# Copying x to the output as two DMAs of alternate 2 KB rows instead of one DMA of long runs

## The reference, cut to what matters

```python
q, k, v = (silu(causal_conv4(n @ W)) for W in (Wq, Wk, Wv))       # n: x, layer-normed
delta   = delta_rule_chunkwise(q, k, v, beta)                      # recurrent state S over the sequence
ms      = multiscale_conv(v, ms_w3, ms_w15, ms_w31, kernel_mix_w, channel_mixer_w)
wts     = softmax(gelu(features @ fusion_w1) @ fusion_w2)
o       = rmsnorm(wts0 * ms + wts1 * delta + wts2 * v)
att     = o @ Wo
ffn     = sigmoid(mix(n) @ W_r) * (square(relu(mix(n) @ W_k)) @ W_v)
out     = x + att + ffn
```

## Time and profile before

| | |
|---|---|
| median of 3 runs | 3813.25 us (3811.24 to 3821.89) |
| the profiled execution, its own time | 3814.92 us |
| its span, first to last instruction | 3813.1 us |
| PE busy | 3381.8 us, 89% |
| DVE busy | 3159.1 us, 83% |
| ACT busy | 2760.3 us, 72% |
| POOL busy | 760.7 us, 20% |
| granted TensorE clock, mean | 0.936 of full speed |
| one step, from one copy of x to the next | 116.86 us in the step read below |

### The profile page before, as it was taken

The page is one execution under the profiler, slowest core; times in us unless marked ns, Lnnn a source line. Parts: engine busy times, 40 slices in busy tenths (PEclk is TensorE's granted clock), DMA queues, the critical chain, the costliest instruction groups (busy, mean ns, idle before and its releaser), DMA issues.

```text
span 3813.1 us, 69963 instructions
## 1 busy us (share of the span) xinstructions
PE 3381.8 (89%) x22848; PEld 2513.9 (66%) x22848; DVE 3159.1 (83%) x7856; ACT 2760.3 (72%) x9144; POOL 760.7 (20%) x1489
## 2 busy tenths in 40 slices
PE   6898889988889888889888898888898888988877
PEld 5666667666667666667666676666666666766654
DVE  5988889888789888798888898888988888888884
ACT  5676778766777667777767776677776777766774
POOL 2012221112221122211122211222112221112220
PEclk8999999999999999999999999999999999999988
DMA  6012211112211122211222111222112221112220
GB/s 176 13 37 47 47 41 36 27 37 47 47 35 35 24 47 47 42 31 25 42 47 47 35 35 24 47 47 42 32 21 46 47 47 32 34 28 47 41 40 7
DMA packets 188307, 154.92 MB, mean 41 GB/s; under 512 B 111804, under 2 KB 146108, under 8 KB 187688
## 3 DMA queue, kind: packets, MB, share of 16 engines
q0 software_dynamic: 31744, 79.70, 12.2%
q1 hardware_dynamic: 156200, 70.76, 7.1%
HBM read 51.34 MB, written 52.95 MB: 27 GB/s over the span
## 4 chain that ended last, share of the span: by engine, by line
PE 48%; ACT 23%; DMA 15%; issue 8%; DVE 4%; POOL 1%; ACTq 0%; POOLq 0%; DVEq 0%; SPq 0%
DMA my<-prod 14%; PE front L516 6%; PE dense L721 6%; PE dense L674 5%; PE dense L678 5%; PE dense L754 5%; PE dense L662 5%; ACT my L1106 3%; DVE my L1531 2%; PE cell L637 2%; PE small L690 2%; ACT dense L1136 2%; ACT prod L1117 2%; PE cell L644 2%; PE cell L645 1%
## 5 line engine op out<-in xcount | busy, mean ns | idle before, releaser
L1531 DVE SCALAR_TENSOR_TENSOR my<-vT,mw,my 128x256 f32<-128x256 f32 x5408 | 2233.9, 481 | 34.8 <-DMA my<-prod 20.2
L516 PE MATMUL front<-xsh,wk 128*128 128x256 f32 x1024 | 291.0, 448 | 252.7 <-ACT raw L894 252.7
L721 PE MATMUL dense<-xsh,w 128*128 128x256 f32 x2048 | 481.9, 381 | 4.0
L516 PEld LDWEIGHTS front<-xsh,wk 128*128 128x128 f32 x1024 | 232.4, 230 | 306.1 <-ACT raw L894 264.1
L1117 ACT ACTIVATE prod<-vT,mw 128x256 f32<-128x256 f32 x480 | 210.6, 509 | 295.5 <-DMA my<-prod 295.4
L397 POOL TENSOR_SCALAR vare<-xsq 128x2 f32<-128x2 f32 x32 | 6.2, 193 | 2096.8 <-ACT xsh L856 2096.8
L721 PEld LDWEIGHTS dense<-xsh,w 128*128 128x128 f32 x2048 | 368.4, 190 | 72.1 <-ACT xr L1168 11.1
L1507 DVE SCALAR_TENSOR_TENSOR xr<-xsh,rest,xr 128x256 f32<-128x256 f32 x128 | 53.7, 482 | 277.4 <-ACT xk L1072 277.4
L1079 ACT ACTIVATE ka<-dense 128x512 f32<-128x512 f32 x64 | 38.2, 597 | 314.7 <-PE dense L662 314.7
L457 POOL DMA_DIRECT2D my<-prod x160 | 146.4, 915 | 540.0 <-ACT prod L1117 341.0
L662 PE MATMUL dense<-xk,wfk 128*128 128x256 f32 x1024 | 236.8, 385 | 12.0 <-DVE xk L1507 10.1
(11 more groups left out here) (182 smaller groups left out, 7021.9 us busy)
## 6 DMA issues: line engine op xcount, KB each, us to landing
my<-prod POOLq DMA_DIRECT2D x160, 384.0 KB, 4.2
xa<-in_x SPq DMA_DIRECT2D x32, 512.0 KB, 4.5
rows_out<-Bm SPq DMA_DIRECT2D x64, 256.0 KB, 4.2
out<-xb POOLq DMA_DIRECT2D x32, 512.0 KB, 6.1
Yq<-units_out SPq DMA_DIRECT2D x128, 32.0 KB, 3.1
w<-in_w SPq DMA_DIRECT2D x1, 2048.0 KB, 16.5
Bu<-rows_out SPq DMA_DIRECT2D x32, 64.0 KB, 3.1
units_out<-Xu SPq DMA_DIRECT2D x32, 64.0 KB, 2.5
```

What stands on the lines that cost most here:

```text
L516: i = e.matmul(by_batch(front[pair % 2][:, c * W:(c + 1) * W]), wt[:, k, hs(c0 + c)], xsh[s % 2][:, k, :, 1:1 + P], start=(k == 0), stop=( ...
L721: e.matmul(by_batch(o), w1[:, k, hs(2 * pair + c)], xsh[s % 2][:, k, :, 1:1 + P], start=(k == 0), stop=False)
L1531: i = e.scalar_tensor_tensor(o, vT[s % 2][:, c, :, off:off + P], mw[:, col:col + 1], o, ALU.mult, ALU.add)
```

## The change

The copy of one step's rows of x is issued as two DMAs instead of one. Each takes both batches, and of the 128 rows of a batch every second one: the first DMA the even rows, the second the odd rows. A row is 512 floats, 2 KB. The place in SP's program is the same. Both DMAs count up the same semaphore by 16, so `add_out` waits for 32 a step instead of 16.

```diff
@@ copy_x
                 if s >= 2:
                     e.wait_ge(stored[s % 2], s // 2 * 16)
-                e.dma_start(out[:, s * P:(s + 1) * P, :], x[:, s * P:(s + 1) * P, :]).then_inc(x_copied[s % 2], 16)
+                def every_second(t):
+                    return t[:, s * P:(s + 1) * P, :].rearrange("b (p t) d -> t b p d", t=2)
+
+                for t in range(2):
+                    e.dma_start(every_second(out)[t], every_second(x)[t]).then_inc(x_copied[s % 2], 16)
@@ add_out
-                e.wait_ge(x_copied[s % 2], s // 2 * 16 + 16)
+                e.wait_ge(x_copied[s % 2], s // 2 * 32 + 32)
```

## The result

The changed kernel takes 3644.93 us (median of 4 runs, 3640.35 to 3666.02), beside 3814.49 for the kernel before; the ratio is 0.9564, 95% interval 0.9524 to 0.9604. That is 170 us less, where 276 were forecast. The profiled execution took 3647.26, 167.7 less than that of before.

What follows compares the result with a forecast made beforehand. The bound was PE's pause while addition r0 took turns with the copy's 64 KB packets on two engines. 28 steps x 9.4 = 263 plus about 13 for the other four, off 3814.9, gave 3539 (3537 against the median); range 3475 to 3650.

Steps and rivals of the forecast that it cites:

- the forecast's own 3488 to 3606: Whole kernel: bounds around the forecast time, from gains of 11.2 and 7.0 us a step; the forecast had chance 0.66.
- rival 1: Copy's queue: short packets stretch the copy, so `Yq` is late or additions r1 and r2 pay more; 3610 to 3790, chance 0.18.
- the longest landing: Sign at the additions of `prod` onto `my`: longest time from issue to landing falls from 15.9 to some 6 us.
- the clock: Sign at PE: without the long pause the granted clock is near 1.00, against 0.94 in the step with it.
- The turn is one packet for one: Copy's two engines: copy's and additions' queues alternate one packet each, even with many small packets waiting.
- r0 ... pays 8 x 0.088 = 0.7 us: First addition onto `my`: 8 rows an engine each wait one 2 KB packet of 0.088 us, on top of 4.2 us.
- its four turns: Addition r0 before the change: 4 copy packets of 64 KB an engine at 2.43 us, 9.7 us on top.
- the other four: The first, two short and the last of 32 steps, outside the 28 with the long pause: about 13 us gained together.
- `Yq`: PE's read of `Yq`: copy ends at 1135.3 as `units_out` is issued at 1135.1, so `Yq` arrives at 1143.1, just when wanted.
- rivals 1 and 2: The second, at L570: copy so slow that PE waits longer for `Yq` than now for `raw`; 3880 or 4168, chance 0.06.
- What is late next: Engines after the pause: ACT waits 0.9 us for r1, PE about 1.0 at L662; 9.4 us a step gained.
- Rival 4: The copy's rows spread over all 16 engines, nothing in the way: 10.1 us a step, 3519 us, chance 0.04.

Runs made afterwards that it cites:

- The halves: Against the kernel before: the copy as two DMAs, each of one half of the rows, in 64 KB packets; 3814.36 us, ratio 0.9989.
- the move of the unchanged copy: Against the kernel before: the same copy, 64 KB packets on two engines, issued by SP behind the reads of `Yq`; 3522.98 us, ratio 0.9246.
- the copy over 16: Against the kernel before: the copy as one DMA of 2 KB rows, the 128 positions outermost, in the old place; 3544.16 us, ratio 0.9282.

## Why the prediction was right, and where it was off

**What bounded the kernel: right.** r0's landing of 15.3 us on the copy's two engines was the pause. The halves (same packets, no change), the 2 KB rows (pause gone) and the move of the unchanged copy (all of it and more gone) show it from three sides. The two engines, read from 1.8 engines' share, are confirmed by the copy over 16.

**In range, but with luck.** 3645 us is 5 us inside the range of 3475 to 3650. It is outside the forecast's own 3488 to 3606 and inside rival 1's 3610 to 3790, and the gain is 170 us where 276 were forecast. That the time still fell in the range is owed to the part that was added to it for rival 1, and the reason why the kernel was slower than forecast stands in neither. Of the signs, the longest landing (9.5, not some 6) and the clock (0.97 over the run, not near 1.00) did not come.

**The turn is one packet for one: right.** Where both queues are being served on the same engines, the trace of the change has 12 packets of each in 2 us. The Trainium skill (DMA: Bandwidth & Descriptors, Queues, rings and completion order) gives about 9 to 17 descriptors before an engine switches. The trace does not agree in that window, nor in the earlier trace rows with 6 and 6, and the measurement decides.

**"r0 ... pays 8 x 0.088 = 0.7 us", and r1 the same: this term was mis-sized.** In the step shown the two landed in 7.4 and 7.2 us where 4.9 each was put down. The turns cost what was said (0.10 us each at most). Two things were missing.

The first is the late start: an addition issued while the copy runs begins on its two engines some 2.6 us after the other 14. The trace of the kernel before has a gap of that size too. Queue 0 there from 1117 to 1120, and from 1120 to 1130.1:

```profile
q0 software_dynamic: 126, 0.34, 59.7%
...
q0 software_dynamic: 18, 0.05, 2.5%
```

These are again 9 packets for each of 14 engines, and then the 18 of the other two. r0's first packets came at 1117.2, the copy's first two at 1117.8, and r0's first two on the copy's engines at 1120.5. The 2.7 us between were one packet of 64 KB, so that the gap looks like a first turn and can't be told from one there. The prediction counted it among its four turns, and so let it shrink with the packet.

The second is the load of x, issued 0.7 us ahead of the copy, which the prediction had left out of r0's landing. With the copy moved and the load where it was, r0 lands in 5.4 us at the median, not 4.2:

```profile
my<-prod POOLq DMA_DIRECT2D x1, 384.0 KB, 5.4
```

(That is the r0 of 1038.51 in the run with 64 KB packets behind the reads of `Yq`.) Of r0's 7.4 us, 4.2 + 1.2 + 0.7 for the turns leave about 1.3 for the late start (an estimate from these figures). At the median of all steps r0 takes 8.3 us, which leaves 2.2.

In the step shown the difference follows from this. Counted from the copy's issue, the product of r2 starts at 16.4 us instead of the forecast's 1128.2 - 1114.71 = 13.5, 2.9 later: 0.6 because r1 is issued later behind ACT's wait of 1.23, 2.3 because r1 takes 7.2. PE's L666 starts at 27.75 instead of 24.8, again 2.9 later, and the gain there is 34.28 - 27.75 = 6.5 instead of 9.5. The step's own gain is 6.6. Over the 28 steps that had the long pause it is 5.9 on average instead of 9.4, 165 in all: this step's wait for r0 is 1.23, where the 26 such waits have 2.3 on average. The steps from the first, second and sixth copy gained 3.6, lost 2.9 and gained 2.2, some 3 together, where 13 were put down for the other four. That makes the 168.

**`Yq`: right that it holds, for a reason a little different.** The forecast had the copy end 20.6 us behind its issue, just as `units_out` is issued. It ended some 17.7 behind it (from 1087.6 on queue 1 had 11 packets left), since r2 comes later and the packets take 0.084 when alone; `units_out` is issued at 23.5. PE does not wait at L574. What rivals 1 and 2 said of this place did not come. Rival 1 also said "r1 and r2 each pay more", as a consequence of a longer copy. The copy was not longer, r2 landed in 4.0 us at the median as before, and it was r0 and r1 that paid more. So the time is inside rival 1's range without its mechanism.

**What is late next: right in kind.** PE's waits moved to L750 (71.9 us, 42 had been there before) and to L666 (28.8 us, 1.0 in the step, as forecast); DVE's wait for ACT is 3.6 in the step, where 0.9 was forecast, 2.7 more, nearly the same 2.9.

**Rival 4** did not come: the two engines stayed, as the outermost count of 2 said. Made on purpose, it gave 3544, 25 above the 3519 at which it was priced.

## What to carry to other kernels

In these traces two queues on one DMA engine take turns packet by packet, so the size of the background transfer's packets is the price that the foreground transfer pays per turn: the copy in DRAM, joined into 64 KB runs, held up a 3 KB packet for 2.4 us each time. Going on from 2 KB to 1 KB gained nothing more; the late start was the same. See on how many engines the transfer runs (the share of 16 engines in a window of the trace), put the long dimension outermost so that it uses all, and, better than either, issue it where nothing that is waited for is in flight: the unchanged copy some 26 us later gained 282 us, where smaller packets in the old place gained 170. Even there it held up a transfer, `add_out`, but one with time to spare. A background transfer that is free by its bytes is not free by its place.

## What was not expected of the hardware

An addition issued by POOL while a copy from SP's queue was running began on the copy's two engines 2.6 to 2.9 us after it began on the other 14, and that did not depend on whether the copy's packets had 1, 2 or 8 KB (139 packets of 1 KB went by, 61 of 2 KB in the first 2.4 us, 17 of 8 KB). What the engines do in that time no view shows, and whether it is a fixed time or a fixed amount under way (about 0.14 MB on two engines) was not tried. A packet from DRAM to DRAM took 0.084 us with 2 KB and 2.43 us with 64 KB, so 2 KB cost 11% more than the same bytes in a long run.
